# Cross attention on one core: TensorE takes a slot's output tile ahead of the next slot's query projection

## What is computed

```python
Q = (query @ w_q.T).reshape(B, S, 16, 32).transpose(0, 2, 1, 3)
K = (key @ w_k.T).reshape(B, -1, 16, 32).transpose(0, 2, 1, 3)
V = (value @ w_v.T).reshape(B, -1, 16, 32).transpose(0, 2, 1, 3)
attn = softmax(einsum('bhqd,bhkd->bhqk', Q, K) / sqrt(32), axis=-1)
ctx = einsum('bhqk,bhkd->bhqd', attn, V).transpose(0, 2, 1, 3).reshape(B, S, 512)
x = ctx @ w_o.T + b_o + query
out = (x - mean(x)) * rsqrt(var(x) + 1e-5) * ln_gamma + ln_beta
```

## Time and profile before

| | before |
|---|---|
| median of 3 runs | 613.66 us (613.42 to 614.11) |
| the profiled execution: time, span | 615.86 us, 614.1 us |
| busy PE / PEld | 585.9 (95%) / 425.7 (69%) |
| busy POOL / DVE / ACT | 480.9 (78%) / 473.2 (77%) / 444.1 (72%) |
| granted TensorE clock, mean | 0.981 |

### The profile page before, as it was taken

One profiled execution on the slowest core, in us unless ns is written; L12 is line 12 of the kernel. 1 busy time (PEld: TensorE's weight loads), 2 busy tenths in 40 slices (PEclk: granted clock), 3 DMA queues, 4 the chain that ended last, 5 costly groups with the idle time before them and its releaser, 6 DMA issues.

```text
span 614.1 us, 8719 instructions
## 1 busy us (share of the span) xinstructions
PE 585.9 (95%) x2602; PEld 425.7 (69%) x2602; DVE 473.2 (77%) x864; ACT 444.1 (72%) x794; POOL 480.9 (78%) x334
## 2 busy tenths in 40 slices
PE   8968789999999999999999999999999999999874
PEld 7745567777777777777777777777777777777553
DVE  7356678888888888888888888888888888888536
ACT  7437777787777877778777787777877778766620
POOL 4336759888898888988889888898888988868740
PEclk9979999999999999999999999999999999999779
DMA  8333413333343334333343233432344321222232
GB/s 311 101 98 85 132 45 98 87 94 113 113 117 86 93 112 118 114 87 91 114 121 115 83 91 115 118 111 86 90 120 117 112 86 50 74 73 74 71 103 86
DMA packets 84223, 63.05 MB, mean 103 GB/s; under 512 B 56752, under 2 KB 56752, under 8 KB 84176
## 3 DMA queue, kind: packets, MB, share of 16 engines
q1 hardware_dynamic: 81936, 62.23, 34.4%
q10 hardware_dynamic: 2240, 0.26, 0.3%
HBM read 39.39 MB, written 16.78 MB: 91 GB/s over the span
## 4 chain that ended last, share of the span: by engine, by line
PE 91%; ACT 2%; DVE 2%; POOL 1%; issue 1%; ACTq 1%; DMA 0%; SPq 0%; DVEq 0%
PE ps_o L280 30%; PE ps_q L280 29%; PE ps_c L280 15%; PE ps_s L334 9%; PE ps_s L344 5%; PE ps_s L280 2%; ACTq L165 1%; ACT probs L476 1%; POOL p_lo L682 1%; PE ps_c L287 1%; DVE z L630 0%; ACT p_hi L409 0%; DMA max_rows<-max_turned 0%; DVE c_raw L605 0%; ACT inverse L483 0%
## 5 line engine op out<-in xcount | busy, mean ns | idle before, releaser
L682 POOL TENSOR_TENSOR p_lo<-probs,p_hi 128x1024 fp32r<-128x1024 f32 x64 | 153.9, 2404 | 53.9 <-ACT p_hi L409 53.9
L576 DVE STREAM_TRANSPOSE turned<-ps_s 128x1024 f32<-128x1024 f32 x64 | 80.0, 1250 | 46.3 <-PE ps_s L334 46.3
L280 PE MATMUL ps_q<-x_hi,wq_lo 128*128 128x512 f32 x256 | 108.7, 425 | 0.0
L280 PE MATMUL ps_o<-wo_hi,c_lo 128*128 128x512 f32 x256 | 104.4, 408 | 2.3 <-POOL c_lo L697 2.3
L470 ACT ACTIVATE inverse<-ps_c 64x512 f32<-64x512 f32 x64 | 38.2, 597 | 89.8 <-PE ps_c L280 89.8
L280 PE MATMUL ps_o<-wo_hi,c_hi 128*128 128x512 f32 x256 | 103.0, 402 | 0.0
L280 PE MATMUL ps_o<-wo_lo,c_hi 128*128 128x512 f32 x256 | 102.9, 402 | 0.0
L280 PE MATMUL ps_q<-x_hi,wq_hi 128*128 128x512 f32 x256 | 102.0, 399 | 0.0
L280 PE MATMUL ps_q<-x_lo,wq_hi 128*128 128x512 f32 x256 | 101.9, 398 | 0.0
L690 POOL TENSOR_TENSOR y<-y,gamma_row 128x512 f32<-128x512 f32 x60 | 77.6, 1293 | 20.4 <-ACT y L512 20.4
L672 POOL TENSOR_TENSOR x_lo<-xT_raw,x_hi 128x512 fp32r<-128x512 f32 x60 | 78.0, 1301 | 18.0 <-ACT x_hi L409 18.0
(11 more groups left out here) (92 smaller groups left out, 1139.4 us busy)
## 6 DMA issues: line engine op xcount, KB each, us to landing
xT_raw<-in_xT SPq DMA_DIRECT2D x64, 256.0 KB, 3.3
x_raw<-in_x SPq DMA_DIRECT2D x64, 256.0 KB, 2.7
out<-y SPq DMA_DIRECT2D x64, 256.0 KB, 2.2
max_rows<-max_turned SPq DMA_DIRECT2D x128, 16.0 KB
ctx_raw<-in_ctxT SPq DMA_DIRECT2D x4, 256.0 KB, 4.2
wk_raw<-in_wkT SPq DMA_DIRECT2D x4, 256.0 KB, 4.4
wq_raw<-in_wqT SPq DMA_DIRECT2D x4, 256.0 KB, 5.9
wv_raw<-in_wvT SPq DMA_DIRECT2D x4, 256.0 KB, 6.8
```

The lines of the kernel that those rows point to most:

```text
L280: mm = nc.tensor.matmul(dst, lhs, rhs, start=(first and n == 0), stop=(last and n == len(passes) - 1))
L576: nc.vector.transpose(turned[:, :], ps_s[:, 2 * s:2 * s + 2, :].rearrange("p b r -> p (b r)")).then_inc(turned_done, 1)
L682: nc.gpsimd.tensor_tensor(p_lo[:, :, :], probs[:, :, :], p_hi[:, :, :].bitcast(fp32), ALU.subtract).then_inc(p_lo_done, 1)
```

## The change

Inside TensorE's slot loop the call `project_output(t - OUT_LAG)` moves up. It stood behind `project_queries(t + 1)` and the two value projections of slots 0 and 1, ahead of `combine_values(t - 1)`; now it stands right behind `start_output(t - OUT_LAG)`, ahead of `project_queries(t + 1)`. The same instructions are issued with the same waits in them. The streams of the other four engines are unchanged.

```diff
                 if t - OUT_LAG >= 0:
                     start_output(t - OUT_LAG)
+                if t - OUT_LAG >= 0:
+                    project_output(t - OUT_LAG)
                 if t + 1 < SLOTS:
                     project_queries(t + 1)
                 if t == 0:
                     project_values(2)
                 if t == 1:
                     pe.wait_ge(values_lo_done, 1)
                     project_values(3)
-                if t - OUT_LAG >= 0:
-                    project_output(t - OUT_LAG)
                 if 0 <= t - 1 < SLOTS:
                     combine_values(t - 1)
```

## The result

| | before | changed |
|---|---|---|
| median | 613.88 us (613.42 to 616.0, 4 runs) | 695.49 us (694.89 to 696.26, 4 runs) |
| profiled execution: time, span | 615.86, 614.1 us | 696.26, 694.4 us |
| busy PE / POOL / DVE / ACT | 95 / 78 / 77 / 72% | 88 / 69 / 67 / 64% |
| granted clock, mean | 0.981 | 0.956 |

The changed kernel is slower by 13.2%: the ratio is 1.132, 95% interval 1.129 to 1.135. The forecast was 697, between 676 and 716.

The account below looks back on a forecast made before the run. The prediction took TensorE to bound the kernel at 8.52 us a slot, with GpSimd and ScalarE close behind. 613.7 plus 65 of waits gave 679 at full clock, plus 18 for clock falls 697, range 676 to 716.

Parts of the forecast that it names:

- The three chains from the last query matmul: From its start: 1.84 us to the next score, 10.03 to the next slot's combine, 6.34 to a chunk's first output matmul.
- the waits for `p_lo`: TensorE waits for GpSimd's `p_lo` before the combine, 1.16 us in two slots of four.
- the chunk at full clock: Four slots walked with their waits: 38.83 us where they were 34.08, so 4.75 more a chunk.
- The output waits: TensorE waits for `c_lo` at a chunk's first output tile: fourteen times, 3.3 us twice and 2.1 twelve times.
- The sum at full clock: Twelve full chunks 57.0, lead-in 4.7, last chunk about 3.5: 65 us more, giving 679.
- the 18 of the forecast: Falls of TensorE's granted clock after output waits: 8 x 2.2 = 18 us, taking 679 to 697.
- GpSimd beside VectorE: GpSimd's steps shift against VectorE's: some 4 us over the kernel at most, kept for the range, not in the sum.
- the `p_lo` chain alone: Rival: the output wait is covered and only `p_lo` delays the combine, 0.68 us a slot, 652; chance 0.07.
- The queries' own chain alone: Rival: only the score after the query product is late, 0.11 us a slot, 620; chance 0.04 shared with no change.
- Not slower: Rival: GpSimd and ScalarE absorb the shift, TensorE stays at 8.52 a slot, 613.7; within 0.2% given 0.02.
- the second chain: Last query matmul through ScalarE and GpSimd's `p_lo` to the next slot's combine: 10.03 us, TensorE there at 8.87.
- the third: Last query matmul through `y`, gamma, beta and `c_lo` to a chunk's first output matmul: 6.34 us, TensorE there at 3.05.

Follow-up runs that it names:

- the run with the waits filled: Changed kernel with eight matmuls of constant weights, results unused, ahead of each of the 14 `c_lo` waits: 679.9 us, ratio 1.105.
- its control: Kernel before the change with `q_hi` moved behind `x_hi` and `y` in ScalarE's stream: 621.4 us, ratio 1.011.
- the run with three early tiles: Kernel before with only three output tiles of a chunk moved ahead of the query projection, the chunk's first tile left behind it: 648.9 us, ratio 1.055.
- with ScalarE reordered: Changed kernel with ScalarE's order at the end of a round as `y`, `q_hi`, `c_hi`, `x_hi`: 622.0 us, ratio 1.012.
- the run without beta: Changed kernel without GpSimd's addition of beta: 659.1 us, ratio 1.072.

## Why the prediction was right

- Which chains: right. The three chains from the last query matmul measured 1.87 to the score (1.84 forecast), 6.32 to the first output tile (6.34), and the waits for `p_lo` came in two slots of four as walked.
- Their sizes: the chunk at full clock was 38.82 against 38.83. Inside it two terms were off against each other: the `p_lo` waits are 0.89 and not 1.16, and the score costs 0.14 and not 0.11, in every slot and not only where nothing else has waited. The output waits were 3.03, twelve near 2.04, and 2.53, against 3.3, twelve at 2.1, and 3.3.
- The sum at full clock: 65 forecast; 66 measured by the run with the waits filled (679.9 less 613.9), 63.4 by the two profiles (80.3 less 16.9).
- The clock: the 18 of the forecast was near the measured 15.6 (695.5 less 679.9) by luck, since two errors offset each other. I took 8 falls at 2.2 us, and there were 11 at 1.54 (16.9 by the profile). The price came from one row of the drain where twelve matmuls in a row were slow; in the steady stretch a fall ends inside the output block: seven of its steps take 0.42 to 0.43 us instead of 0.23 (from 159.70 to 162.69 at t = 14), the last two are fast again. The count rested on comparing lengths of waits (1.76 and 2.25). That step failed, though the sum came out near: waits of 1.35 to 1.43 brought falls too, waits of 1.76 none, and a wait of 2.25 did in the kernel before and didn't in its control, so the length of the wait doesn't decide by itself.
- GpSimd beside VectorE: the four short steps took 1.28 to 1.30 us in the changed kernel too (1.283, 1.284, 1.300 and 1.292 on average for gamma, beta, `c_lo` and `x_lo`), and `p_lo` 2.39. The 0.04 us between median and longest in the earlier trace rows are 3.5%, and not the 5% that I wrote. The Trainium skill ("GPSIMD Engine Reference", section "Key points") warns of contention with VectorE instructions that have two SBUF inputs or run in a 2-port perf mode. No slowing is to be seen here, but it is hardly a test: VectorE's long two-input instructions (`c_raw`, `q_lo`, `z`) each take one input from PSUM, where TensorE's products lie (`ps_c`, `ps_q`, `ps_o`).
- The rivals: the `p_lo` chain alone (652) does exist and is near what the run with three early tiles shows, 648.9. The queries' own chain alone (620) is what remains with ScalarE reordered, 622.0. "Not slower" needed the second chain at 8.87 and the third at 3.05; the third measured 6.32.

## What to carry to other kernels

Where a block of a busy engine is moved, ask first what it stood in front of: its length was the cover of every chain that begins with the block it now precedes. Follow such a chain through the in-order streams of the other engines and count all that is queued behind the first reader, buffer-reuse waits included, and not the reader alone. Walk the period over as many slots as the waits repeat in (four here); an average slot shows neither wait.

## What the runs showed of the hardware

TensorE's granted clock fell to the lower of its two levels (1.2 for 2.4 GHz) after waits as short as 1.35 us (the run without beta), with nine matmuls on 64 rows or fewer ahead of them, and after 1.39 to 1.43 us where two on 128 rows stood between those and the wait. It stayed up through the waits of 1.70 to 1.77 us behind twelve matmuls on 128 rows in slots 2 to 5 of every trace. Waits of 2.25 us behind such a block went both ways: a fall in the kernel before, none in its control with `q_hi` moved. So no length of wait in these runs separates fall from no fall. Eight added matmuls on 128 rows removed all eleven falls, eight on 8 rows with the same columns none. A fall cost 1.5 us in the steady stretch and 2.2 us at the last `c_lo` wait of the drain; eleven of them are some 16 of the 82 us.
